# Graph attention on one core: rounds of three chunks with three row buffers in place of six, and sums added two chunks later in place of three

## The reference, cut to what matters

```python
def _gat(x, src, dst, W, a_src, a_dst, bias, n_nodes):
    H, C = a_src.shape
    xw = (x @ W).reshape(n_nodes, H, C)
    al_s = jnp.einsum('nhc,hc->nh', xw, a_src)
    al_d = jnp.einsum('nhc,hc->nh', xw, a_dst)
    logits = jax.nn.leaky_relu(al_s[src] + al_d[dst], LRELU_SLOPE)
    m = jax.lax.stop_gradient(jax.ops.segment_max(logits, dst, num_segments=n_nodes))
    e = jnp.exp(logits - m[dst])
    denom = jax.ops.segment_sum(e, dst, num_segments=n_nodes)
    alpha = e / denom[dst]
    out = jax.ops.segment_sum(alpha[:, :, None] * xw[src], dst, num_segments=n_nodes)
    return out.reshape(n_nodes, H * C) + bias
```

## Time and profile before

| | us |
|---|---|
| median of 3 runs (5954.24 to 5956.43) | 5954.8 |
| profiled execution, its own time | 5958.3 |
| its span, first to last instruction | 5956.3 |
| attention loops of layers 0, 1, 2, first to last gather's start | 2306.3 to 3415.6, 3529.6 to 4641.5, 4755.9 to 5863.2 |
| GpSimd busy | 3822.0 |
| VectorE busy | 2667.4 |
| TensorE busy | 2547.3 |
| ScalarE busy | 508.0 |

### The profile page before, as it was taken

One profiled execution on the slowest core, in us unless ns is written; L12 is line 12 of the kernel. 1 busy time (PEld: TensorE's weight loads), 2 busy tenths in 40 slices (PEclk: granted clock), 3 DMA queues, 4 the chain that ended last, 5 costly groups with the idle time before them and its releaser, 6 DMA issues. The chain is left out here.

```text
span 5956.3 us, 52364 instructions
## 1 busy us (share of the span) xinstructions
PE 2547.3 (43%) x7810; PEld 1679.5 (28%) x7810; DVE 2667.4 (45%) x7267; ACT 508.0 (9%) x1859; POOL 3822.0 (64%) x3789
## 2 busy tenths in 40 slices
PE   0000000000069985656566665655555644444443
PEld 0000000000023333434344444433343433333333
DVE  5534454455640004555555535555555333333333
ACT  2200000000000012000000030000000300000001
POOL 1477787788810015777777737777777377777774
PEclk9855555555588887777777687777777755555555
DMA  7200000000055543444444515444444232222222
GB/s 271 67 3 3 4 3 4 4 3 4 5 210 233 232 163 77 111 109 109 109 109 109 104 53 109 109 109 109 109 109 109 36 57 56 56 57 56 56 56 28
DMA packets 338667, 493.49 MB, mean 83 GB/s; under 512 B 248114, under 2 KB 249911, under 8 KB 325626
## 3 DMA queue, kind: packets, MB, share of 16 engines
q0 software_dynamic: 150096, 317.52, 22.9%
q1 hardware_dynamic: 172715, 131.66, 7.0%
q10 hardware_dynamic: 15824, 43.96, 1.9%
HBM read 438.14 MB, written 55.12 MB: 83 GB/s over the span
## 5 line engine op out<-in xcount | busy, mean ns | idle before, releaser
L465 POOL DMA_INDIRECT rows_all<-gat_tab,ell x2664 | 2517.7, 945 | 821.3 <-issue 627.3
L920 PE MATMUL banks<-rows_all,ident 128*128 128x264 f32 (+1 forms) x5328 | 1803.7, 508 | 1557.0 <-PEq L107 1557.0
L920 PEld LDWEIGHTS banks<-rows_all,ident 128*128 128x128 f32 x5328 | 1303.6, 285 | 2056.3 <-issue 1869.0
L469 POOL DMA_INDIRECT adj_t<-post_w,post_i x876 | 1068.9, 1220 | 298.2 <-issue 293.3
L814 PE MATMUL banks<-x_t,h_st 128*64 128x512 f32 (+1 forms) x532 | 211.0, 554 | 1455.0 <-PEq L107 1455.0
L1384 DVE COPY lrel<-m_all 128x8 f32 x666 | 137.7, 207 | 1525.3 <-DMA rows_all<-gat_tab,ell 1203.8
L1409 DVE TENSOR_TENSOR rows_all<-rows_all,banks 128x1024 f32<-128x1024 f32 (+1 forms) x666 | 685.0, 1042 | 136.4 <-DVE ex_in L1397 136.4
L814 PEld LDWEIGHTS banks<-x_t,h_st 128*64 128x64 f32 x532 | 72.1, 139 | 1591.4 <-issue 1591.4
L741 ACT ACTIVATE banks<-ex_in 128x40 f32<-128x40 f32 x666 | 138.3, 208 | 3076.8 <-ACTq L107 3076.8
L465 POOL DMA_INDIRECT x_res<-x_d,node_i x26 | 24.5, 943 | 543.8 <-DMA x_d<-x_res 536.2
L1362 DVE TENSOR_TENSOR acc<-acc,banks 128x264 f32 (+1 forms) x675 | 259.5, 384 | 45.2 <-DVEq L107 12.4
(11 more groups left out here) (254 smaller groups left out, 2172.3 us busy)
## 6 DMA issues: line engine op xcount, KB each, us to landing
x_t<-adj_t SPq DMA_DIRECT2D x18, 3200.0 KB, 10.4
y_t<-adj_t SPq DMA_DIRECT2D x18, 3200.0 KB, 10.4
rows_all<-gat_tab,ell POOLq DMA_INDIRECT x2664
adj_t<-rows_all ACTq DMA_DIRECT2D x25, 1600.0 KB, 23.5
adj_t<-post_w,post_i POOLq DMA_INDIRECT x876, 2.1
ell<-ell_d SPq DMA_DIRECT2D x666, 2.5 KB
x_t<-adj_t SPq DMA_DIRECT2D x2, 1600.0 KB, 6.5
x_t<-key_d SPq DMA_DIRECT2D x1, 1664.0 KB, 6.4
```

The lines of the kernel that those rows point to most:

```text
L465: return g.indirect_dma_start(out=dst, out_offset=None, in_=table, in_offset=bass.IndirectOffsetOnAxis(ap=idx, axis=0))
L469: return g.indirect_dma_start(out=table, out_offset=bass.IndirectOffsetOnAxis(ap=idx, axis=0), in_=data, in_offset=None)
L920: last = t.matmul(sum_ps[u % SUMS][:, 0:width], ident[:, :], rows[u][:, r * width:(r + 1) * width], start=(r == 0), stop=(r == SLOTS - 1))
```

## The change

Two constants change. `RING` sets three things at once: the number of row buffers and index buffers, the number of chunks in a round, and the divisor of the number of rounds. `LAG` sets how many chunks after its own `weigh` a chunk's sum is added, and how many tile numbers are kept over the end of a round.

```diff
 SORT_TILES = EP // P
-RING = 6
+RING = 3
 TILE_AT = SLOTS
 ...
 SUMS = 3
-LAG = 3
+LAG = 2
 STRIP = 512
```

## The result

The changed kernel takes **7082.3 us** (median of 4 runs, 7075.2 to 7088.1) against 5955.4 us: a ratio of **1.189**, 95% interval 1.187 to 1.191. The direction and the mechanism are those of the forecast; the time lies 177 us above the forecast of 6905 and 2 us outside its range.

The account below looks back on a forecast made before the run. GpSimd's gather pace bounds the kernel before; with three buffers, late returns make a loop of waits through all engines. +408, +408 and +133 us for layers 0, 1 and 2 on 5958.3 give 6907, about 6905 us; range 6430 to 7080.

Parts of the forecast that it names:

- The bound before: Attention loops before the change: GpSimd issues a gather every 1.25 us, never waits for a buffer, and other engines wait.
- the lateness and the threshold: Row buffer returns 13.9 us after its chunk's last gather starts, at full clock; three buffers want it after 11.25 us.
- Steps 1, 2, 3 and 5 of the round: Round of layers 0 and 1: 3.25 us to TensorE; 0.38 to add; 2.26 plus 0.15 to TensorE again; 6.75 to weigh.
- The 57 us more: Gather's landing, by the skill page's 2.31 us behind issue instead of the trace's 2.05: 219 rounds later, near 6960 us.
- Step 4: Buffer release at TensorE's end to chunk 1's first gather of the next round: 0.6 us, ends 0.38 and 1.25.
- The clock: TensorE's matmuls in layers 0 and 1, partly at low clock: c0 = 3.7 us for chunk 0, c1 = 3.4 for chunk 1.
- Landings: Gathered rows arriving before weigh: 3.0 us from last gather's start, plus 0.3 us a round for late ones.
- Layer 2: Loop with rows of 136 floats: no waiting add, rounds of 17.0 us, 1241 against 1108 us, so +133 us.
- Rounds and padding: Each layer's loop: 73 rounds gather exactly 219 chunks where 37 gathered 222, saving 3 padding chunks, 15 us.
- the index load: Index load of chunk k+3, released at weigh(k)'s end: stays covered and costs nothing; uncovered, some 3 us a round.
- the ends of rounds: VectorE's 2.29 us between a round's last multiply and next weigh: twice as many ends, but they fit and cost nothing.
- a rival of 0.12: Layers 0 and 1: clock down, c0 = c1 = 3.86 us, release to gather 1.25; 7140 us in all, chance 0.12.

Follow-up runs that it names:

- e2: Kernel before with three row buffers in rounds of three, LAG left at 3: 6898.0 us against 5959.5, ratio 1.157.
- e7: Changed kernel with GpSimd counting `rows_free` down after a chunk's gathers, not before them: 7005.9 us, beside 6673.9 for the kernel before.
- e13: Kernel before with rounds of six kept, but three row buffers used twice a round, and LAG 2: 7348.0 us against 5960.9, ratio 1.233.
- e1: Kernel before with LAG 2 alone, all six buffers kept: 6362.6 us against 5959.5, ratio 1.069.
- e15: Changed kernel with the multiply ahead of the next weigh and `rows_free` counted down after the gathers: 6015.2 us against 5960.9, ratio 1.009.
- e14: Changed kernel with a chunk's multiply ahead of the next weigh: 6093.7 us against 5960.9 for the kernel before, ratio 1.022.
- e16: Kernel before with five buffers, LAG 3, and `rows_free` counted down after the gathers: 5926.3 us against 5960.9, ratio 0.995.
- e6: Changed kernel with GpSimd's wait for a row buffer ahead of its index wait and `tile_known` signal: 7169.5 us, beside 6673.9 for the kernel before.
- e10: The changed kernel run again unedited: 7103.3 us, beside 6620.6 for the kernel before, ratio 1.073.
- e8: Changed kernel with extra unread matmuls filling TensorE's pauses: 6871.8 us, beside 6673.9 for the kernel before.
- e9: The kernel before run again unedited, with a profile: 6622.0 us, beside 6620.6.
- e4: Kernel before with five buffers in rounds of five, LAG 3: 5929.2 us against 5959.5, ratio 0.995.
- e12: Changed kernel with multiply ahead of the next weigh and `rows_free` counted down after the gathers: 6557.1 us, beside 6620.6 for the kernel before, ratio 0.991.
- e5: Changed kernel with a chunk's multiply ahead of the next weigh: 6701.2 us, beside 6673.9 for the kernel before, ratio 1.005.
- e11: Changed kernel with a chunk's multiply ahead of the next weigh, run again: 6661.4 us, beside 6620.6 for the kernel before, ratio 1.006.

## Why the prediction was right in kind and wrong in size

- **The bound before, the lateness and the threshold.** Right, but for one gather before that did wait for a buffer (below). 13.9 us against 11.25 was said; e2 gives the buffers alone 939 us, with four buffers (16.25 us) 46 us are left over the kernel before, and with five (21.25 us) nothing.
- **Steps 1, 2, 3 and 5 of the round.** Each is in the timeline after: 3.25 (3013.73 - 3010.48), 0.38 (3017.97 - 3017.59), 2.26 (3019.01 + 1.22 - 3017.97), 2.97 from the last gather to weigh. In the other rounds of layers 0 and 1 the first three are the same within 0.1 us. That the way leads through the add and not through chunk 0's buffer is shown by e2. The 57 us more that were estimated from the Trainium skill ("DMA: Bandwidth & Descriptors", the anatomy of one DMA) are not borne out: the step takes 3.0 us in the median, as in the trace before, and its mean of 3.2 to 3.3 us is within the 0.3 us that the sum had for late landings.
- **Step 4, release to first gather: the step that failed.** I took 0.6 us, by likeness to TensorE's own next matmul, with 0.38 and 1.25 as ends. It is 1.19 us in nearly every round (1.18 to 1.30 in layers 0 and 1), once on the way: 0.59 x 219 = 129 of the 177 us missed. What the count-down adds between the wait and the gather is 0.52 of it in layers 0 and 1 (e7). "Nothing in the trace waits for `rows_free`" was wrong. One gather of the kernel before does, in layer 1, behind the very matmuls of the earlier trace rows from which I took the 0.38 us:

```profile
3558.46 0.95 POOL L465 DMA_INDIRECT rows_all<-gat_tab,ell  x1 [0.30 <-issue]
3562.52 0.94 POOL L465 DMA_INDIRECT rows_all<-gat_tab,ell  x1 [3.11 <-POOLq L107]
```

TensorE's matmuls end at 3557.46 + 3.86 = 3561.32, and the gather starts 1.20 us later. The price stood in the trace, in one place out of 2664, and with it the forecast would have been 7034.
- **The clock.** c0 = 3.7 and c1 = 3.4 were near, and a little low: over all rounds the trace gives 3.81 and 3.50 in layer 0, 3.81 and 3.44 in layer 1. That is 26 us.
- **Landings, and a pause that stood in no sum.** The starts of all instructions on the way, in the 72 rounds of layer 0 that are followed by another, give the mean round: 3.25 + 3.81 + 0.38 + 2.26 + 0.15 + 3.50 + 1.19 + 3.95 + 3.22 = 21.71 us. The last term is the landing, for which the sum had 3.0 + 0.3. The one before it is a chunk's four gathers, for which it had 3.75. In every ninth round GpSimd stops ahead of the second gather of chunk 1:

```profile
2505.98 0.94 POOL L465 DMA_INDIRECT rows_all<-gat_tab,ell  x1 [2.06 <-POOLq L107]
2509.06 0.94 POOL L465 DMA_INDIRECT rows_all<-gat_tab,ell  x1 [2.14 <-issue]
```

This comes 8 times a layer, always 108 gathers apart, and takes 1.84 us more than the usual 0.30 (one shorter, in layer 2): 44 us in all. In the kernel before no gather stops inside a chunk. The profile shows nothing that is waited for; the cause is open. In e7 seven of the eight pauses of layers 0 and 1 are 0.29 us over the usual.
- **Layer 2.** +133 forecast, +197 measured: 43 us are step 4, 14 us the pauses, and 7 us are open.
- **The sum of it.** 129 us of step 4, 44 of pauses and 26 of the clock are 199 us too little; the program saved 24 us outside the loops that were not foreseen. That gives 175 of the 177 us; smaller terms nearly cancel.
- **Rounds and padding, the index load, the ends of rounds.** Right: 2628 gathers, no gather behind an index load, e13 slower with half the rounds.
- **The range.** Its upper end took 0.6 us for step 4 into the likely case and left 1.25 to a rival of 0.12, although 1.25 was a bound of a cost that I held to be unknown, and no less likely than 0.38. With it the range would have reached 7220.
- **What I had not seen:** I gave LAG no price without the lack of buffers. e1 shows that LAG 2 costs 403 us by itself, since 2.79 + 3.86 us a chunk is over GpSimd's 5.0. The terms 0.38, 2.26 and 0.15 stood in the prediction, and adding them as a cycle of their own would have shown it.

## What to carry to other kernels

Count a buffer's way back in time, from its last write to its release, and compare it with the time until it is wanted again: number of buffers less one, times the pace, plus one step. Well below that the time is flat (five and six buffers here), above it every microsecond counts once a round, and near it late landings cost a little (four buffers); and often an order within one engine (here a multiply behind the next chunk's first step) is the longest term and cheaper to change than buffers. Do the same sum for every loop of waits that an edit shortens, those between two engines too, with the slowest clock and not the mean. Before you price a wait by its likeness to another, search the whole trace for one instance of it: one gather of 2664 had it here. If there is none, carry the whole bound in the range. Where a wait is on the way, try the bookkeeping behind the work (e15 took 79 us less than e14 by it; layer 2 of e7 won only 6 us, and e16, where hardly a buffer is waited for, nothing).

## What the runs showed of the hardware that was not expected

- **A count-down between GpSimd's wait and an indirect gather costs 0.52 us** in layers 0 and 1 (1.19 against 0.67 us), three further semaphore steps ahead of it, a count-down among them, 0.17 us together (e6, e7).
- **GpSimd stops for 2.14 us once in 108 gathers** when it waits for buffers in rounds of 12 gathers (changed kernel, e10), with nothing in the profile that it waits for, and never does so inside a chunk in the kernel before.
- **A low clock can hold itself down.** In the stretch of e1 the slower matmuls lengthen the cycle to 6.65 us, TensorE is busy 3.86 us of it, and two chunks on end take the 3.86 us of the lower level; the loop's mean is 0.64. With TensorE's pauses filled it is 0.93 (e8, on the changed kernel). That the one sustains the other is read from these two and not tested by itself.
- **The same program at 5955 and at 6620 to 6674 us.** In e9, layer 0's gathers take this long, which answers to the earlier trace rows:

```profile
L465 POOL DMA_INDIRECT rows_all<-gat_tab,ell x888: 943/949/990, 2315.7 to 3644.8; - x178
```

That is 5.99 us a chunk and not 5.0; layer 2, with half the bytes a row, has 5.98. Runs on the chip numbered 2 show both times (5960 us beside e1 to e4, 6621 us beside e9 to e12), so it is not shown to be a property of one chip. The timeline shows engines pausing together without one of the waits known so far ("issue" is time in which nothing that the profile shows was waited for):

```profile
3004.23 2.02 PE L920 MATMUL banks<-rows_all,ident 128*128 128x264 f32 x8 [0.60 <-PEq L107]
...
3005.05 1.22 DVE L1409 TENSOR_TENSOR rows_all<-rows_all,banks 128x1024 f32<-128x1024 f32 x1 [0.25 <-DVE ex_in L1397]
...
3012.16 0.43 DVE L1362 TENSOR_TENSOR acc<-acc,banks 128x264 f32 x1 [5.07 <-issue]
...
3012.42 3.86 PE L920 MATMUL banks<-rows_all,ident 128*128 128x264 f32 x8 [6.17 <-issue]
...
3013.00 0.94 POOL L465 DMA_INDIRECT rows_all<-gat_tab,ell  x1 [2.75 <-issue]
```

The multiply ended at 3006.27 and TensorE's chunk before it at 3006.25, but the next begins at 3012.42; VectorE's add (3012.16) and the next gather (3013.00) start within 0.9 us of each other. Kernels at 5 us a chunk suffer (e5, e9, e11, e12), the changed kernel at 7.2 us a chunk hardly (7103 against 7082). What holds TensorE there, late instructions or something else, no run here tells; it stays open.
